# A graph-network kernel on one core: the point in a batch at which GpSimd requests the next tile's edge records

## The reference, cut to what matters

```
attn = jnp.einsum('bnhd,bmhd->bnmh', q, k) * scale
attn = attn.at[b_idx, loc_src, loc_dst].add(eb)        # layer 0
msg  = h[row] * norm[:, None]                          # layers 1 and 2
out  = jax.ops.segment_sum(msg, col, num_segments=n)
msgs = support[col] * edge_vals[:, None]               # layer 3
```

## Time and profile before

| what | value |
|---|---|
| median of three runs | 1416.37 us |
| profiled execution, and its span | 1415.81 us, 1414.4 us |
| TensorE busy in the span | 1363.3 us (96%) |
| VectorE busy | 885.8 us (63%) |
| ScalarE busy | 568.1 us (40%) |
| GpSimd busy | 79.0 us (6%) |
| fetches by GpSimd in build_pool (L713) | 14, in 7 pairs, first at 57.0 us, last at 331.0 us |
| build stage, 50 to 434 us (384 us): TensorE, VectorE, ScalarE busy | 361.4, 350.5, 234.5 us |

### The profile page before, as it was taken

How to read it: one execution, slowest core, us unless ns; L and a number is a source line. 1 busy time by engine, 2 the same in 40 slices (tenths; PEclk the granted TensorE clock), 3 DMA queues, 4 the chain that set the end, 5 groups by cost and what they waited for, 6 DMA issues and landing times.

```text
span 1414.4 us, 26661 instructions
## 1 busy us (share of the span) xinstructions
PE 1363.3 (96%) x11273; PEld 840.9 (59%) x11273; DVE 885.8 (63%) x1380; ACT 568.1 (40%) x980; POOL 79.0 (6%) x86
## 2 busy tenths in 40 slices
PE   7788999989998999999999999999999999999998
PEld 6688898879997665544444444454444445444443
DVE  6898998999997886657655766542244323432322
ACT  2575666555654447611142112312253324422322
POOL 3130000000001210000000100002100000000000
PEclk9899999999999999999999999999999999999999
DMA  9634344334437741200001000012201232553201
GB/s 324 225 101 138 120 159 130 117 127 133 148 131 281 227 148 41 74 30 1 1 0 51 10 0 0 1 45 86 64 19 57 61 82 62 214 209 104 89 1 60
DMA packets 71333, 136.92 MB, mean 97 GB/s; under 512 B 11908, under 2 KB 24324, under 8 KB 69798
## 3 DMA queue, kind: packets, MB, share of 16 engines
q1 hardware_dynamic: 68542, 123.98, 26.5%
q0 software_dynamic: 1280, 5.77, 1.5%
q10 hardware_dynamic: 1384, 5.38, 1.1%
HBM read 81.79 MB, written 53.32 MB: 96 GB/s over the span
## 4 chain that ended last, share of the span: by engine, by line
PE 80%; DVE 14%; ACT 3%; issue 2%; DMA 1%; another core or an unknown queue 0%; ACTq 0%; DVEq 0%
PE banks L2277 31%; PE banks L2211 13%; PE banks L2341 11%; PE banks L1228 5%; DVE x_sb L866 4%; PE banks L1627 3%; PE banks L1182 2%; PE banks L1165 2%; PE banks L1239 2%; DVE x_sb L851 2%; PE banks L1139 1%; PE banks L2155 1%; DVE x_sb L859 1%; PE banks L1597 1%; PE banks L1240 1%
## 5 line engine op out<-in xcount | busy, mean ns | idle before, releaser
L2277 PE MATMUL banks<-g,count 128*128 128x512 f16 x1024 | 227.6, 379 | 0.5 <-DVE tiles L2543 0.5
L2277 PE MATMUL banks<-count,g 128*128 128x512 f16 x1024 | 223.6, 379 | 0.0
L2211 PE MATMUL banks<-w_parts,h_parts 128*128 128x512 f16 x960 | 215.3, 379 | 1.7 <-DVE g L2492 1.4
L2277 PEld LDWEIGHTS banks<-count,g 128*128 128x128 f16 x1024 | 99.6, 98 | 118.0
L2277 PEld LDWEIGHTS banks<-g,count 128*128 128x128 f16 x1024 | 99.8, 98 | 113.5 <-DVE tiles L2543 1.0
L2341 PE MATMUL banks<-g,part 128*128 128x512 f16 x768 | 165.9, 379 | 0.0
L2211 PEld LDWEIGHTS banks<-w_parts,h_parts 128*128 128x128 f16 x960 | 91.1, 98 | 115.4 <-issue 11.4
L866 DVE TENSOR_TENSOR x_sb<-eb_parts,x_sb 128x4096 f16<-128x4096 f16 x64 | 145.7, 2277 | 0.0
L1228 PE MATMUL banks<-x_sb 128*128 128x128 f16 x2048 | 127.8, 222 | 14.0 <-DVE x_sb L866 13.8
L1228 PEld LDWEIGHTS banks<-x_sb 128*128 128x128 f16 x2048 | 121.4, 99 | 18.2 <-DVE x_sb L866 17.1
L2341 PEld LDWEIGHTS banks<-g,part 128*128 128x128 f16 x768 | 75.1, 98 | 90.6
(11 more groups left out here) (343 smaller groups left out, 1886.0 us busy)
## 6 DMA issues: line engine op xcount, KB each, us to landing
weight_dram<-w_new SPq DMA_DIRECT2D x60, 256.0 KB, 2.7
count<-weight_dram SPq DMA_DIRECT2D x29, 512.0 KB, 7.3
qk_dram<-stage SPq DMA_DIRECT2D x64, 128.0 KB, 2.4
tiles<-x_dram SPq DMA_DIRECT2D x32, 256.0 KB, 3.5
x_dram<-tiles SPq DMA_DIRECT2D x32, 256.0 KB, 2.8
count<-in_x SPq DMA_DIRECT2D x4, 1024.0 KB, 11.6
h<-in_x SPq DMA_DIRECT2D x16, 256.0 KB
h_dram<-h_t SPq DMA_DIRECT2D x8, 512.0 KB, 2.9
```

The source lines that it names most:

```text
L2211: mm = pe.matmul(out, m.h_parts[:, slot, zh, k], m.w_parts[:, zw, k], start=n == 0 and layer != 3, stop=n == len(passes) - 1)
L2277: mm = pe.matmul(m.agg_ps[:, b], lhs, rhs, start=i == 0 and z == 0, stop=i == NT - 1 and z == 1)
```

## The change

The fetch for tile t, from t = 2 on, waits for one more thing: the semaphore `batch` at 8(t-2)+4, which is raised when the last count-and-weight product of batch number 8(t-2)+3 has been done. That is the same batch in which `read` allows the fetch. The fetch for tile 1 is not touched. The wait is added in both branches.

```diff
 def build_pool(nc, io, keep, m, s, first_round):
     pool = nc.gpsimd
     records = io["rec_dram"].rearrange("e f -> (e f)").unsqueeze(1)
     if not first_round:
...
     for t in range(1 if first_round else 0, GTILES):
         if t > 0:
             pool.wait_ge(s["read"], FGROUPS * t)
+        if t > 1:
+            pool.wait_ge(s["batch"], NBATCH * (t - 2) + 4)
         for z in range(2):
             pool.indirect_dma_start(keep.gathered[:, z, :], None, records,
...
```

## The result

The changed kernel takes 1406.19 us in the median of four runs (1403.04 to 1407.57) and the kernel before, beside it, 1416.33 us (1416.25 to 1417.41). The ratio is 0.9924, with a 95% interval of 0.9906 to 0.9941: 10.1 us faster. Its profiled execution took 1407.57 us, with a span of 1406.2 us against 1414.4. All source lines of the build lie three further down: L1142 is the L1139 of before, L989 is L986, L849 is L846, L977 is L974, L1231 is L1228, L1243 is L1240, L716 is the fetch.

The account below looks back on a forecast made before the run. It took the build's TensorE-led chain, with `batch` released late beside five fetches, as the bound. Gains of 3.8 us plus 0.5 for the clock made 4.3, so 1416.37 became 1412.1 us, range 1407.6 to 1416.8.

Parts of the forecast that it names:

- The cause: Build stage, five fetches: while GpSimd works off a fetch, TensorE's `batch` is seen late, by 1.44 to 2.18 us.
- the place without a fetch: Control, fourth batch of tile 6: no fetch follows, and ScalarE starts 0.19 us after L1139's start.
- the held case: Behind the moved fetch, `chunk` is held to the end of the same 2.07 us: 3.8 us gained, chance 0.50.
- an estimate: Place at 187 us: the new fetch was put at 188.21, with `batch` seen at 187.97.
- The rival "not held": Nothing of TensorE's is held behind the moved fetch: 6.85 us, with the clock 7.9 to 9.3 us, chance 0.25.
- The clock: Bias products after TensorE's idle time at 303.78 us: shorter idle time may return 1.05 us; half counted, 0.5.
- Places 3 and 4: Late releases at 233 and 283 us: gains of 0.10 and 1.44 us if held, 1.44 each if not.
- The caps: TensorE's idle time until the next place limits the gain: 1.38 us at 187 us, 0.41 at 330 us.
- The move of tile 2's fetch: Fetch at 89.97 us, with no late release seen beside it: its move costs nothing, give or take 0.4 us.
- The data is not missed: Fetched records are read a tile, 47 us, later, so delaying the fetch some 0.9 us costs nothing directly.
- The slower rival: Fetch waits out VectorE's 4.7 us one-hot run and holds `chunk`: net 3.4 us slower, 1419.8 us, chance 0.10.
- The row held against the Trainium skill's rule: Tile 2's second half beside L851 took 1.16 us instead of 0.94, read as running side by side without full blocking.

Follow-up runs that it names:

- g1: Kernel before without the fetches of tiles 3 to 7 (records stay those of tile 2), on chip 4: 1404.23 us, ratio 0.9925.
- g4: Kernel before with only each fetch's second half waiting for `batch`, first half at its old place, on chip 4: 1409.93 us, ratio 0.9966.
- h0: Kernel before, unchanged, run and profiled on chip 12: 1404.82 us, ratio 0.9997.
- g2: Changed kernel but with the wait for `batch` alone, in place of that for `read`, on chip 4: 1404.89 us, ratio 0.9939.
- halves: Kernel before with only each fetch's second half waiting for `batch`: 1405.81 us on chip 15, 1405.69 on chip 1, 1409.93 on chip 4.
- g0: Kernel before, unchanged, run and profiled on chip 4: 1415.48 us, ratio 1.0007.
- b_again: Kernel before, unchanged, run and profiled anew on chip 5: 1415.49 us, ratio 1.0009.
- e3: Kernel before with each fetch released by the next batch's bias products alone, on chip 15: 1404.1 us, ratio 0.9997.
- f2: Changed kernel but with the wait for `batch` alone, in place of that for `read`, on chip 1: 1405.2 us, ratio 0.9993.
- h2: Kernel before with the fields turned ahead of the 32 bias products in the fourth batch, on chip 12: 1409.11 us, ratio 1.0024.
- one_wait: Changed kernel but waiting for `batch` alone, in place of `read`: 1405.23 us on chip 15, 1405.2 on chip 1, 1404.89 on chip 4.
- h1: Kernel before with 3, 1, 2, 4 and 6 small GpSimd clearings ahead of the fetches of tiles 3 to 7, on chip 12: 1404.98 us, ratio 0.9997.
- h3: Kernel before with plain GpSimd DMAs in place of indirect fetches for tiles 3 to 7, on chip 12: 1405.32 us, ratio 1.0004.
- next_bias: Kernel before with each fetch released by the next batch's bias products alone: 1404.1 us on chip 15, 1405.62 on chip 1.
- f3: Kernel before with each fetch released by the next batch's bias products alone, on chip 1: 1405.62 us, ratio 1.0001.

## Why the prediction was wrong, step by step

- **The cause was right.** The late release goes with the fetch, and with the fetch moved or left out the whole gain is there. The kernel without the fetches (g1) and the one with half of them early (g4) show it, beside the changed kernel. It was read from the place without a fetch, which was as good a control as the trace held; that a fetch can stand at its old place with the release on time (h0) it could not show.
- **Held or not held: the step that failed.** The prediction said "I take the held case, because the row nearest to it, `batch` itself 0.6 us into the fetch, was held every time". `chunk` was held nowhere. In the changed kernel the fetch starts at 0.91 us behind L1142's start (187.92 - 187.01) and not at 0.43 as "an estimate" had it, so `chunk`, raised at 0.69, was already up. But with one wait, where the fetch did start first, `chunk` was not held either (g2). So the reason failed and not only the estimate. The held case put 0.45 in place of 2.18 and 0.10 in place of 1.44, 3.07 us too little. The rival "not held", with a chance of 0.25, gave 7.9 to 9.3 us and has the mechanism that happened; even its far end, 1407.1, is 0.9 us above the 1406.19 measured, and the range was cut at 1407.6.
- **The clock was mis-sized.** The term was 0.5 us, for one place. Places 3 and 4 gave 1.52 and 0.81 us more than the release. The rows of TensorE that answer to the last two of the earlier trace rows:

```profile
252.74 1.96 PE L1231 MATMUL banks<-x_sb 128*128 128x128 f16 x32 [1.96 <-DVE x_sb L869]
...
297.14 1.96 PE L1231 MATMUL banks<-x_sb 128*128 128x128 f16 x32 [2.94 <-DVE x_sb L869]
```

  The 32 products take 1.96 us at both, where they took 3.37 and 3.01: 1.41 and 1.05 us. The idle times right before them are what they were (1.96 and 2.94), while the prediction had the second shrink to 1.49: VectorE's run up to that place came earlier as a whole, and TensorE's work with it. Five microseconds of each kernel, before and then after, columns as above, tell it by the clock:

```profile
255.00:260.00 5.00, 3.62 (x43) 3.63 (x44) 5.00 (x6) 0.25 (x2) 0.00 (x0) 0.67 0.22 79
...
305.00:310.00 5.00, 5.00 (x70) 4.77 (x69) 4.66 (x6) 2.32 (x5) 0.00 (x0) 0.71 0.42 134
```

```profile
255.00:260.00 5.00, 5.00 (x76) 4.72 (x72) 5.00 (x7) 3.58 (x8) 0.00 (x0) 1.00 0.22 79
...
305.00:310.00 5.00, 4.66 (x80) 4.18 (x80) 5.00 (x7) 2.52 (x5) 0.00 (x0) 1.00 0.43 160
```

  0.67 and 0.71 before: for part of these windows TensorE ran at 1.2 GHz; 1.00 after is 2.4 GHz throughout. In halves (g4) the same two windows still have 0.73 and 0.96, with a release late by 0.77 us. Late release and low clock go together, but not strictly. Of the five stretches, all four traces with a late release have two with a low clock (places 3 and 4 in before, g0 and g4, places 1 and 4 in b_again). Of the fifteen traces without it that keep the order of TensorE's work, two have one, at place 4 (e3 and f2, 0.69 and 0.77 us longer than the others there), and thirteen none. And the same 1.95 us of idle time stands ahead of products at either level. The bias products in the stretches behind places 1 and 3 in b_again, and behind place 4 in f2, where no release is late:

```profile
160.59 3.55 PE L1228 MATMUL banks<-x_sb 128*128 128x128 f16 x32 [1.95 <-DVE x_sb L866]
...
257.54 1.96 PE L1228 MATMUL banks<-x_sb 128*128 128x128 f16 x32 [1.95 <-DVE x_sb L866]
```

```profile
294.23 3.36 PE L1230 MATMUL banks<-x_sb 128*128 128x128 f16 x32 [2.94 <-DVE x_sb L868]
```

  So the 2.33 us are measured, and the low clock beside them; that the late release makes the clock fall is likely by the counts and not shown.
- **The caps were too tight.** At places 2 and 5 TensorE's idle time was to cap the gain at 1.38 and 0.41; 1.46 and 0.86 came. In the fifth stretch the busy time itself fell, 40.89 to 40.50, perhaps since products that overlap are counted once. Idle time in a busy column is not a strict cap. Nor does a late release cost its whole length there: late by 0.79 us in halves (g4), it cost nothing at place 5, whose stretch has the changed kernel's 42.91 us.
- **What else was right.** The move of tile 2's fetch was worth nothing (46.89 and 46.90 us). The data is not missed, and the stages behind keep their length. The slower rival, the fetch shut out by VectorE's whole run, did not come.
- **The row held against the Trainium skill's rule was misread.** The prediction set the second half of tile 2's fetch (99.89, 1.16 us) beside L851, which starts after it. The instruction in which it starts is L849, 99.81 to 100.23, with 0.34 us left. At the five places a half that takes 0.94 us alone takes longer by what is left of the VectorE instruction with two inputs in which it starts, less some 0.12 us: 0.20 left gives 1.01, 0.34 gives 1.16 (g2), 1.18 and 1.67 give the 2.00 and 2.50 of the changed kernel. It ends 0.82 us behind that instruction. The Trainium skill, SBUF — State Buffer, section Who interferes with whom, calls the shared port an exclusive lock, for which the order of issue decides who blocks. For a fetch that starts inside a VectorE instruction the trace agrees. For one that starts first it does not: L853 starts 0.44 us into the first half in g2 and takes its 1.22 us as ever. The wait was for one instruction and not for the run of five, and nobody waited for the fetch. The first half of tile 2's fetch is the exception: it took 9.62 us while VectorE's instructions followed one another without a wait, and the prediction gave no reason. Whenever it began (8.27 us long in the changed kernel, 4.34 in e3, 13.37 in h2), it ended 0.10 to 0.12 us behind the start of VectorE's next L846. So its end goes with VectorE's work; by what, no run shows.
- **What could not have been seen.** One trace does not tell that the late release belongs to some chips. Of the six groups it was there in three (the first pair's, whose chip was not noted, chips 5 and 4); on chip 12 it was absent in the kernel before itself, and on chips 15 and 1, where the kernel before was not profiled, it took 1405 us, and halves had no late release with its first half at the old place. The changed kernel itself was run in two of the three, and was faster in both; where the kernel before takes 1405 us only its close relative one_wait was run (chips 15 and 1), and made no difference.

Open: why a release is late on some chips and not on others, and why `batch`, raised about 0.6 us into a fetch, is held on chip 4 while `chunk`, 0.27 us into one, is not. Open too is whether the fetch needs the turning of the fields or idle engines beside it to hold a release. The scan of distances (h1), the plain transfer (h3), the early turning (h2) and next_bias (e3, f3) were made for that, and met only chips without the effect.

## What to carry to other kernels

When two idle engines start at the same moment, well behind the instruction that should release them, look for what else ran in that gap, and for a place in the same trace where it did not run; then move it behind the release and price the move by the places, once as if nothing takes its turn and once as if something does, keeping the whole of both in the range. Add the clock at every stretch that shows it below 1.00, not at one. Before a trace's row is held against a rule, look which instruction was running when the row began. And before an edit is called worthless or good, run the kernel before on the same chip and on another: here one_wait is worth 10 us on chip 4 and nothing on chips 15 and 1.

## What the runs showed of the hardware that I had not expected

- The same program has two times, 1405 and 1415 us, by the chip or the session: on chip 4 ScalarE sees TensorE's release 1.6 to 2.3 us behind L1139's start beside an indirect fetch of GpSimd, on chip 12 after 0.18 us beside the same fetch at the same distance.
- The hold grows with the fetch: at places 2 to 4 it lasts 1.37 to 1.39 us from its start with one half ahead, 2.06 to 2.10 with two (g4, g0); at places 1 and 5, 1.40 and 1.42 against 2.74 and 2.76.
- A wait more on GpSimd is not free: behind two waits the fetch starts 0.72 us after `batch` is seen by the others (187.92 - 187.20), behind one 0.23 (184.94 - 184.71 in g2), and so in every trace of the two kernels.
- Half a fetch of GpSimd takes 0.94 us alone, and ends 0.82 us behind the VectorE instruction with two inputs in which it starts: 1.01, 1.16, 2.00 or 2.50 us in all. VectorE's instructions that start during it keep their time to 0.05 us.
